# Four cross-attention layers on one core: which groups at the end normalise their small layers behind the values, and new order tables for both ends

## The reference

```
# layer 0
q, k, v = x @ Wq, ctx @ Wk, ctx @ Wv                  # inner width 1024
probs   = softmax(q k^T / 8 + col_bias)               # 16 heads, 64 x 64 each
x       = probs v @ Wo + bo + x
# layers 1, 2, 3
xn      = x * rsqrt(mean(x*x) + 1e-5) * norm_w
q, k, v = xn @ wq, ctx @ wk, ctx @ wv                 # 16 x 8, 4 x 8, 4 x 8
attn    = softmax(q k^T / sqrt(8))
x       = x + (attn v) @ wo
```

## Time and profile before

| | us |
|---|---|
| median of 3 runs | 1392.41 (1391.6 to 1392.94) |
| the profiled execution, its own time | 1390.16 |
| its span in the trace | 1388.3 |
| PE busy | 1364.2 |
| DVE busy | 1063.7 |
| ACT busy | 1001.8 |
| POOL busy | 724.3 |

### The profile page before, as it was taken

How to read it: one execution, slowest core, us unless ns; L and a number is a source line. 1 busy time by engine, 2 the same in 40 slices (tenths; PEclk the granted TensorE clock), 3 DMA queues, 4 the chain that set the end, 5 groups by cost and what they waited for, 6 DMA issues and landing times.

```text
span 1388.3 us, 59323 instructions
## 1 busy us (share of the span) xinstructions
PE 1364.2 (98%) x25656; PEld 1056.5 (76%) x25656; DVE 1063.7 (77%) x2239; ACT 1001.8 (72%) x2204; POOL 724.3 (52%) x840
## 2 busy tenths in 40 slices
PE   8999999999999999999999999999999999999997
PEld 6777777778777777777777777777777777777765
DVE  3488777987777977778877778877779776787776
ACT  3577777767777777777677777677777676776775
POOL 5355446655446555556545556554466544564332
PEclk9999999999999999999999999999999999999998
DMA  5000010010010100100110001100100000010000
GB/s 148 21 26 18 19 32 17 26 27 23 27 29 16 27 27 23 27 24 21 26 27 23 28 17 27 26 23 27 28 17 26 26 23 26 18 29 26 10 19 14
DMA packets 46004, 37.04 MB, mean 27 GB/s; under 512 B 17072, under 2 KB 41520, under 8 KB 45744
## 3 DMA queue, kind: packets, MB, share of 16 engines
q1 hardware_dynamic: 44576, 32.89, 8.7%
q10 hardware_dynamic: 1168, 0.36, 0.1%
HBM read 16.42 MB, written 4.19 MB: 15 GB/s over the span
## 4 chain that ended last, share of the span: by engine, by line
PE 91%; DVE 4%; ACT 2%; POOL 1%; issue 1%; DMA 0%; POOLq 0%; DVEq 0%; ACTq 0%
PE psum L942 17%; PE psum L930 16%; PE psum L997 10%; PE psum L1015 8%; PE psum L957 8%; PE psum L979 7%; PE psum L1043 7%; PE psum L1007 5%; PE psum L968 5%; PE psum L1051 4%; PE psum L1020 3%; PE psum L949 2%; PE psum L1026 1%; POOL E L889 1%; DVE st L1213 1%
## 5 line engine op out<-in xcount | busy, mean ns | idle before, releaser
L889 POOL TENSOR_TENSOR E<-E,st 128x512 f32<-128x512 f32 x476 | 485.4, 1044 | 169.7 <-DVE st L1225 160.8
L1124 ACT ACTIVATE E<-E,inv 128x512 f32<-128x512 f32 x384 | 273.6, 723 | 140.3 <-DVE E L1217 136.8
L1213 DVE TENSOR_REDUCE st<-psum 128x8 f32<-128x512 f32 x372 | 240.2, 673 | 144.0 <-PE psum L979 143.9
L1222 DVE TENSOR_REDUCE st<-E 128x8 f32<-128x512 f32 x476 | 313.3, 664 | 34.3 <-ACT E L1117 27.2
L1129 ACT COPY E<-psum 128x512 f32<-128x512 f32 x512 | 275.8, 608 | 39.6 <-PE psum L997 39.5
L942 PE MATMUL psum<-wv,cT 128*128 128x374 f32 (+1 forms) x768 | 273.3, 486 | 0.0
L1217 DVE TENSOR_TENSOR E<-psum,st 128x512 f32<-128x512 f32 x372 | 248.0, 677 | 0.5
L930 PE MATMUL psum<-cT,wk 128*128 128x256 f32 x1024 | 242.2, 385 | 4.8 <-DMA wk<-in_L_xattn_Wk 4.8
L901 POOL TENSOR_TENSOR nt<-nt,powers 128x2 f32<-128x2 f32 (+1 forms) x102 | 20.0, 196 | 427.0 <-DVE nt L1252 406.0
L930 PEld LDWEIGHTS psum<-cT,wk 128*128 128x128 f32 x1024 | 192.7, 191 | 39.7 <-issue 5.5
L942 PEld LDWEIGHTS psum<-wv,cT 128*128 128x128 f32 x768 | 138.3, 189 | 72.4 <-ACT V L1085 8.5
(11 more groups left out here) (63 smaller groups left out, 1623.4 us busy)
## 6 DMA issues: line engine op xcount, KB each, us to landing
KB<-K SPq DMA_DIRECT2D x1536, 8.0 KB
cT<-in_ctx_t SPq DMA_DIRECT2D x32, 256.0 KB, 2.7
xq<-in_x_t SPq DMA_DIRECT2D x32, 128.0 KB, 2.1
out<-xT SPq DMA_DIRECT2D x30, 128.0 KB, 1.8
wk<-in_L_xattn_Wk SPq DMA_DIRECT2D x3, 256.0 KB, 5.7
wv<-in_L_xattn_Wv SPq DMA_DIRECT2D x2, 374.0 KB, 8.8
wq<-in_L_xattn_Wq SPq DMA_DIRECT2D x1, 512.0 KB, 7.7
wo<-in_L_xattn_Wo SPq DMA_DIRECT2D x1, 512.0 KB, 4.3
```

Of the source, the lines that this page charges most:

```text
L889: e.tensor_tensor(E3, E3, wide(stat[s][u][:, 16:24]), ALU.mult).then_inc(g_nrm.sem, 1)
L1124: e.activation(E[s][u][:, :], E[s][u][:, :], ACT.Exp, scale=inv[s][:, u // 2:u // 2 + 1]).then_inc(a_exp.sem, 1)
L1213: e.tensor_reduce(stat[s][u][:, 0:8].rearrange("p (r h) -> p r h", r=2), scores_of[g, l, u], AX, ALU.max).then_inc(d_max.sem, 1)
L1222: e.tensor_reduce(stat[s][u][:, 8:16], heads(E[s][u][:, :]), AX, ALU.add).then_inc(d_sum.sem, 1)
```

## The change

Two edits. `LATE` loses group 29: it now holds 30 and 31, the same as `SPLIT`. Group 29's three small layers so get 12 `sum`, 12 `rcp` and 12 `nrm` steps and three copies `pv` on ACT, and lose three `lr`, three `lm` and the ones matmuls of three `pv` steps. And all five tables of the ends are new numbers; the tables of the middle and `PERIOD` are the same. Of the tables the diff shows a line or two.

```diff
 SPLIT = range(NG - 2, NG)
-LATE = range(NG - 3, NG)
+LATE = range(NG - 2, NG)
...
     29: {
-        "s": {0: (-372.47498, -373.06937), 1: (-333.86668,), 2: (-332.76941,), 3: (-329.01806,)},
+        "s": {0: (-374.55636, -374.84232), 1: (-333.7345,), 2: (-331.48934,), 3: (-316.47544,)},
```

More of the change, by code:

```diff
@@ L138 @@
-    2: {
[L139 to L150, removed]
+        "k": {0: (-570.1934, -580.40739, -579.11772, -564.41745)},
@@ L160 @@
[L160 to L164, removed]
+        "k": {0: (-412.71099, -395.62776, -394.66559, -374.46511)},
+        "v": {0: (-372.72927, -370.61535, -348.22122, -356.11236, -372.30535, -369.1062)},
+        "k3": {0: (-372.90485,)},
@@ L222 @@
     0: {
[L223 to L230, removed]
@@ new lines @@
+        "rcp": {0: (-137.47236, -113.56261, -132.13608, -116.19418),
+                1: (-91.08876, -86.19179, -89.36363, -81.97208),
+                2: (-46.92841, -45.5702, -45.7502, -45.34553),
+                3: (-13.75903, -10.80597, -10.5483, -11.08521)},
+        "wo0": {0: (-110.63922,)},
+        "ssq": {1: (-103.28116,), 2: (-64.63156,), 3: (-19.7432,)},
+        "sub": {1: (-99.33518, -95.72384, -100.37059, -90.90692),
+                2: (-63.82851, -63.81404, -57.36626, -57.69001),
+                3: (-17.74498, -14.68705, -11.10967, -15.8716)},
@@ new lines @@
+        "wo": {1: (-65.14174,), 2: (-26.04387,), 3: (1.20324,)},
+    },
+    1: {
+        "add": {0: (-123.9347, -124.08678, -129.90673, -123.76773)},
+        "max": {0: (-122.94758, -120.277, -127.79561, -116.55176),
+                1: (-86.95412, -84.08831, -85.586, -87.24054),
+                2: (-50.68976, -47.80124, -50.00623, -49.29786),
+                3: (-20.79907, -16.40857, -20.32533, -21.63928)},
+        "sum": {0: (-109.56435, -115.36529, -121.76716, -107.48523),
+                1: (-84.2169, -71.586, -77.33131, -76.18611),
+                2: (-44.85429, -38.8769, -46.23005, -41.88022),
+                3: (-15.96003, -14.05217, -11.72302, -15.5517)},
+        "rcp": {0: (-108.55, -111.79223, -116.75733, -107.19357),
+                1: (-79.23267, -69.27373, -77.05579, -73.05612),
+                2: (-41.52825, -35.67586, -37.73781, -34.39427),
+                3: (-15.57518, -13.04692, -10.85911, -15.42494)},
+        "wo0": {0: (-97.11607,)},
+        "ssq": {1: (-87.40507,), 2: (-50.21379,), 3: (-20.68479,)},
+        "sub": {1: (-85.40072, -78.57631, -85.08611, -80.73016),
+                2: (-49.58415, -43.66062, -48.29832, -46.53934),
+                3: (-20.65549, -15.95003, -17.36151, -18.25983)},
+        "wo": {1: (-52.85685,), 2: (-25.75863,), 3: (1.58911,)},
+    },
@@ new lines @@
+    2: {
+        "add": {0: (-125.00087, -127.96467, -110.96922, -117.21148)},
+        "max": {0: (-119.41386, -126.83699, -110.61359, -114.88569),
+                1: (-80.77251, -77.36808, -80.76251, -78.02624),
+                2: (-52.90039, -50.13762, -48.88648, -52.30961),
+                3: (-17.54048, -14.17674, -18.32869, -20.92914)},
+        "sum": {0: (-109.88771, -112.34774, -104.48662, -109.20516),
+                1: (-74.54322, -73.46766, -76.87662, -73.30215),
+                2: (-43.22138, -42.78236, -40.86048, -41.8672),
+                3: (-12.50896, -9.63891, -15.73797, -16.99949)},
+        "rcp": {0: (-101.77915, -103.54262, -103.48137, -107.37561),
+                1: (-73.64324, -71.5386, -75.74443, -72.25362),
+                2: (-42.62136, -38.6697, -36.87089, -41.30804),
+                3: (-11.17836, -9.44817, -10.77329, -12.44155)},
+        "wo0": {0: (-87.96723,)},
+        "ssq": {1: (-82.76127,), 2: (-49.52819,), 3: (-21.7854,)},
+        "sub": {1: (-77.72878, -75.99509, -78.89842, -74.64384),
+                2: (-44.4824, -47.01066, -45.56456, -44.01011),
+                3: (-14.35218, -13.56357, -17.52208, -18.55758)},
+        "wo": {1: (-59.21614,), 2: (-25.45345,), 3: (-0.58643,)},
@@ new lines @@
+        "rcp": {0: (-104.92446, -105.49258, -107.51115, -109.19792),
+                1: (-74.89787, -72.11912, -71.50952, -71.91384),
+                2: (-41.67219, -39.83839, -39.84773, -39.70967),
+                3: (-15.36463, -12.73953, -16.29754, -18.44923)},
+        "wo0": {0: (-86.18902,)},
+        "ssq": {1: (-83.32454,), 2: (-50.24509,), 3: (-24.8951,)},
+        "sub": {1: (-77.16932, -76.55559, -81.29049, -76.87909),
+                2: (-43.51573, -44.14919, -47.61057, -45.25074),
+                3: (-20.69381, -16.96058, -22.09157, -20.31366)},
@@ new lines @@
+        "rcp": {0: (-107.83466, -103.21956, -107.60565, -103.25657),
+                1: (-73.64364, -76.65952, -76.70846, -73.65549),
+                2: (-39.7802, -39.1794, -41.92883, -44.3778),
+                3: (-12.69913, -13.21266, -27.34814, -11.75657)},
+        "wo0": {0: (-86.17302,)},
+        "ssq": {1: (-82.473,), 2: (-56.19583,), 3: (-31.58413,)},
+        "sub": {1: (-78.9105, -79.99844, -80.20947, -77.72271),
+                2: (-48.95112, -53.36949, -46.59744, -53.97666),
+                3: (-28.42518, -29.12043, -30.57306, -28.28955)},
@@ L447 @@
+        "wo": {1: (-60.52534,), 2: (-33.90176,), 3: (-6.46393,)},
+    },
+    30: {
+        "add": {0: (-119.73685, -115.4075, -113.77137, -115.42269)},
+        "max": {0: (-119.40304, -112.72534, -110.51458, -115.2617),
+                1: (-87.12356, -82.76218, -82.15785, -80.61917),
+                2: (-52.78586, -52.49299, -50.16509, -48.69694),
+                3: (-28.56632, -27.39744, -26.74683, -20.93565)},
+        "sum": {0: (-114.74466, -104.85282, -106.13363, -109.76719),
                 1: (None, None, None, None),
@@ L542 @@
+        "ms": {1: (-91.15777,), 2: (-50.95076,), 3: (-24.42034,)},
+    },
+    30: {
+        "sub": {0: (-130.91655, -115.56676, -114.29391, -117.52034),
+                1: (None, -82.44013, None, -78.69196),
+                2: (None, -42.18242, None, -34.45383),
+                3: (None, -14.61606, None, -6.62883)},
+        "nrm": {0: (-98.25636, -102.43145, -102.66071, -115.55281),
                 1: (None, None, None, None),
```

608 lines of the change are left out of this document (272 added, 336 removed), and 84 rows, old and new, of tables (DVE_ENDS, PE_ENDS).

## The result

The changed kernel takes 1386.13 us (median of 6 runs, 1385.16 to 1389.44), the kernel before 1392.68 beside it (6 runs, 1391.6 to 1395.83). The ratio is 0.9958, 95% interval 0.9946 to 0.9971: about 5.8 us faster, and surely by more than 0.2%. The profiled execution took 1385.33 us with a span of 1383.5, against 1390.16 and 1388.3: 4.8 us less, where the sum had said 3.15.

A forecast was written before the change was run, and what follows sets the result against it. PE was taken to bound the kernel up to about 1340 us, then the chains of groups 30 and 31. Start +1.1 and end -4.25 (ones matmuls -2.7, order -1.55) sum to -3.15 us: 1392.41 to 1389.2, range 1386.3 to 1392.4.

The forecast's parts named there:

- The view of the bound: Up to about 1340 us PE sets the time; behind that the chains of groups 30 and 31 do.
- Group 29's nrm: Group 29's transposes must wait for nrm on POOL; the walk found it ready, no more than 0.1 us lost at t(29,2).
- nothing gained: Rival: nrm a microsecond late at each of group 29's three transposes, the 2.7 us gain goes, 1391.9 us; chance 0.25.
- The start, +1.1: Second v step ahead of s(0,0) makes t(0,0) about 1.1 us later, nothing giving it back; bounds +0.2 and +1.5.
- To the end of wo0(31,0,0): From 1339.9 to 1336.4 us, the start aside: two ones batches, s(30,2,1) moved behind it, waits 1.1 us less.
- the walk: Changed order followed from 1250 us on, with profiled durations and 0.1 to 0.15 us between engines.
- From there to the end, -0.75: wo0(31,0,0) to the last wo: 45.6 us before, 44 to 46 forecast; whole end -4.25 us, scores of layer 3 4.5 earlier.
- The end order: lm(31,3,0) behind lr(31,3,1) and lm(31,3,1): the first half's wo comes last, ending 0.25 us later than the last wo did.
- The clock: Granted clock falls from 1.00 to 0.50 behind the wait for the last exp, at the same price as before.
- The sum: Whole kernel: +1.1 - 4.25 = -3.15 us, 1387.0 on the profiled execution, 1389.2 as median.
- more than forecast: Rival: the start costs nothing or the clock holds, 1.1 to 2 us more go, -5.4, 1387.0 us; chance 0.17.
- Slower: Rival: in the last stretch DVE steps with late inputs hold up those behind, +8.0, 1397.2 us; chance 0.08.

The follow-up runs named there:

- the edit in the old order: Kernel before with LATE cut to two groups, the new steps of group 29 placed in the old order: 1400.81 us (ratio 1.006).
- the new start: Order of groups 0 to 2 as in the changed kernel, a second v step ahead of the scores; changed kernel again 1384.96 us (0.9962) and 1385.9 (0.9974).
- the pair above: Profiles of the changed kernel and of it with tables of before for groups 0 to 2 and lm(31,3,0) ahead of lr(31,3,1), 1385.14 us (0.995).
- the first and third set: Sets of four follow-up kernels, each beside the kernel before; the unaltered changed kernel took 1384.96 us (0.9962) in the first, 1385.9 (0.9974) in the third.
- both halves of the change alone: LATE edit in the order of before: 1400.81 us (1.006); changed kernel's order with LATE back at three groups: 1398.41 us (1.0048).
- the step of PE moved: Changed kernel with k(28,0,3) ahead of k(29,0,0) in TensorE's order: 1388.19 us (0.9978).
- the last kernel of the third set: Changed kernel with the order of before in groups 0 to 2, load of context 29 as in the change: 1384.61 us (0.9959).
- the old start: Changed kernel with the tables of before for groups 0 to 2: 1384.21 us (0.9954), and 1384.61 (0.9959) when run again.

## Why the prediction was right, and where it was not

**The view of the bound.** Right. The three ones steps taken off a saturated PE came through at full length, 2.7 us in the stretches as forecast.

**Group 29's nrm.** Right. The three transposes don't wait for POOL, so the rival "nothing gained" is out; the edit in the old order shows that it was a real one, and that the order is what keeps it away.

**The start, +1.1.** The mechanism is right, the size 0.94 by the wait ahead of t(0,0), and 0.25 to 1.3 us in the time. The scores stand 1.25 us later in PE's order of steps, where the prediction had 1.36 (16.44 to 19.05 against 17.05 to 18.41), and from there to the first nrm 0.3 us are given back for its 0.2. In the profile after it is hidden: t(0,0) comes 0.3 us later and not 1.1, because PE without that wait would have come at 32.00 and not at 32.62. The first matmul began at 4.52 us there and at 4.78 before, and the rest is the landing of the following weights. With the new start t(0,0) stood anywhere from 32.93 to 34.82, with the old from 32.30 to 33.20. That is chance and not the change.

**To the end of wo0(31,0,0).** The term was -3.5 without the start. From 1125 us, where the changed kernel's profile is 0.1 us later than that of before, to 1336.28 it gained 3.7. But the close fit is in part luck. Two things that I hadn't foreseen nearly cancel: the wait of 0.89 us for the load of context 29, and a stall of 0.98 us of before that isn't there after (last section). The prediction counted 0.7 us of waits of before between 1140 and 1280; it is 1.07, and this stall is nearly all of it. And the walk's loss from 1255 us on, 1.6 us, is 0.9, since its two waits for ACT came to 0.24.

**From there to the end, -0.75.** Mis-sized. The last wo begins 44.3 us behind the end of wo0(31,0,0), within the forecast's 44 to 46, where 45.6 passed before: -1.3. No single step carries it. Counted from the end of wo0(31,0,0), q(31,2,0) is 0.4 us ahead of the walk, s(31,2,1) 0.3, q(31,3,0) 0.6 and s(31,3,1) 0.7, and of this 0.2 are lost behind the scores. The end order costs 0.29 us by the pair above, for the 0.25 of the walk.

**The clock.** It fell as forecast: 0.72 and then 0.50 behind the wait of 2.05 us, and t took 1.12 us. The rival's part on a clock that holds is out. That the chip, by the Trainium skill, is throttled unless activity holds the clock up (TensorE: Matmul & The Clock Gate, What's actually happening) fits this, and the last section has a case that the row alone wouldn't have led me to expect.

**The sum.** In the profiles: start +0.3 for +1.1, the first 1125 us -0.2, from there to wo0(31,0,0) -3.7 for -3.5, the rest -1.3 for -0.75; -4.9 for -3.15. Of the 1.75 us between them 0.8 is the start's, 0.6 the last stretch's. By their medians the result and the first and third set put the change at -6.55, -6.35 and -4.5 us; the profiles say 4.8. Why before's median lies 2.5 us above its profiled execution in the result, and after's only 0.8, stays open. The outcome lies nearer to "more than forecast" (1387.0) than to the forecast, though neither of the reasons that I gave for that rival held: the start did cost, and the clock did fall. Its price was added up wrong besides: with the larger of its two terms, 2 us, it is -5.15 and 1387.3. And in the prediction's reading of the windows 2.1 us of the idle 12.1 follow the last matmul, not 2.4, since the window ends at 1388; nothing rests on it.

**Slower.** Out for this order, and real for others: both halves of the change alone gave it, though not by the places that the rival named. They lost it at group 29's transposes and `wo`, and through the clock.

## What to carry to other kernels

Where an engine is full, price a step taken off it at its own length, and spend the effort on whether its replacement on another engine arrives in time: here an edit that was worth 6 us in an order made for it cost 9 in the order made for the old one. Before you move a step of the full engine to cover a late transfer, look at the queue that issues the transfer; a place in that queue moves no buffers (0.9964 of before here, and 0.9978 with the step of PE moved). Count more than its length for a long wait of the full engine: behind waits of 1.7 to 3 us the granted clock fell to 0.50 here, and a step behind one took 2.70 us where it takes 1.42. Differences of about 1 us between two profiles of a kernel this long are often the landing of the first weights or a stall of instruction issue, so compare stretches between steps, not absolute times.

## What the runs showed of the hardware that was not expected

**Stalls of issue have a fixed place and a varying length.** PE sometimes stops inside a step for nothing that the profile shows. Timelines of PE, first of the changed kernel as run in the first set:

```profile
51.69 1.98 PE L966 MATMUL psum<-KT,QT 64*64 64x64 f32 x120
55.27 0.34 PE L966 MATMUL psum<-KT,QT 64*64 64x64 f32 x8 [1.60 <-issue]
```

In the changed kernel's first profile there was none at this place, in that of the third set 1.22 us, behind the same matmul; five of the eight profiles with the new start have it. With the old start the longest one has another place, in t(25,2); of the kernel before:

```profile
1139.58 0.90 PE L997 MATMUL psum<-ident,E 64*128 64x64 f32 x21
1141.46 0.59 PE L997 MATMUL psum<-ident,E 64*128 64x64 f32 x11 [0.98 <-issue]
```

It was 0.56 to 1.54 us in all six profiles with the old start, and nothing in the eight with the new. Between 40 and 1330 us such stalls make 3.9 us before, 3.3 after, and 2.2 to 4.6 over all runs. What PE waits for there no view shows.

**The clock can fall where the waits are short.** Windows of PE in the last kernel of the third set, and in that set's first:

```profile
1350.00:1355.00 5.00, 4.05 (x117) 1.00 0.07 15
1355.00:1360.00 5.00, 4.50 (x77) 0.59 0.02 6
1360.00:1365.00 5.00, 4.75 (x166) 0.73 0.01 3
```

```profile
1355.00:1360.00 5.00, 4.63 (x179) 1.00 0.03 8
```

Ahead of it PE had waited 0.42, 0.43 and 0.35 us and stalled for 0.43. The changed kernel's first profile has waits of 0.40, 0.43 and 0.36 and a stall of 0.53 there, and its clock held at 1.00. This profiled run took 1386.59 us, the longest of its five (the others 1383.63 to 1384.94): a loss of some 2 us that looks like chance, in an end with many small waits. The edit in the old order has a fall of this kind too, 0.66 from 1370 to 1375 us, behind waits of 0.52 and 0.38 and a stall of 0.34.

**The first weights.** The first matmul began between 4.39 and 4.78 us, and t(0,0) moved over 2.5 us (32.30 to 34.82) between profiles, of which the order explains 0.94.
